# Second aggregation of a graph network layer on one Trainium2 core: the normed rows turned by DMA instead of by TensorE

## The reference, cut to what matters

```
xn = layernorm(x)
x2 = x + gnn(xn, edges) + mix(xn)       # gnn: x @ W0 + b0 + mean_of_neighbours(x) @ W1 + b1, twice
xf = layernorm(x2)
logits = xf @ Wg + bg + bias            # 6250 x 8
top2 -> softmax -> combine
out = x2 + sum over the two experts e of combine[e] * (relu(xf @ W1[e] + b1[e]) @ W2[e] + b2[e])
```

## Time and profile before

| | us |
|---|---|
| median of 3 runs | 2406.96 |
| lowest and highest | 2403.34 to 2407.14 |
| the profiled execution's own time | 2408.94 |
| span of the profile | 2407.4 |

### The profile page before, as it was taken

How to read it: one execution, slowest core, us unless ns; L and a number is a source line. 1 busy time by engine, 2 the same in 40 slices (tenths; PEclk the granted TensorE clock), 3 DMA queues, 4 the chain that set the end, 5 groups by cost and what they waited for, 6 DMA issues and landing times.

```text
span 2407.4 us, 53368 instructions
## 1 busy us (share of the span) xinstructions
PE 2129.6 (88%) x15340; PEld 1320.2 (55%) x15341; DVE 1612.2 (67%) x4900; ACT 1202.9 (50%) x2425; POOL 360.4 (15%) x427
## 2 busy tenths in 40 slices
PE   2555557999999999999799997999999998699997
PEld 2444445555555555555355553444444444599996
DVE  5999999799999999999443342445444455355554
ACT  2445455355555555555545552444444444366664
POOL 1000000000000000000111110111211112266665
PEclk9665667899999999999899998999999999799998
DMA  2111112522222222222222123555555554655553
GB/s 76 44 34 34 34 37 62 167 115 118 109 117 109 120 110 116 117 109 117 102 75 77 50 85 145 193 185 208 187 194 199 186 206 167 165 91 94 87 93 47
DMA packets 132541, 275.61 MB, mean 114 GB/s; under 512 B 30478, under 2 KB 85951, under 8 KB 130291
## 3 DMA queue, kind: packets, MB, share of 16 engines
q1 hardware_dynamic: 104275, 221.29, 26.3%
q0 software_dynamic: 25216, 44.98, 8.5%
q10 hardware_dynamic: 2976, 8.46, 1.1%
HBM read 137.14 MB, written 132.95 MB: 112 GB/s over the span
## 4 chain that ended last, share of the span: by engine, by line
PE 67%; issue 14%; DVE 8%; DVEq 4%; POOLq 2%; POOL 1%; DMA 1%; ACT 1%; ACTq 1%; SPq 0%
PE bank L2107 44%; PE bank L2098 6%; PE bank L2328 6%; PE bank L2313 6%; POOLq L771 2%; DVE big L1027 2%; DVE big L1041 1%; DVEq L1056 1%; DVEq L1024 1%; PE bank L2295 1%; DVEq L1037 1%; PE bank L2115 1%; DVE big L1039 1%; PE bank L1976 1%; DVE R L1000 1%
## 5 line engine op out<-in xcount | busy, mean ns | idle before, releaser
L2107 PE MATMUL bank<-RW,big 128*128 128x512 f16 (+1 forms) x4900 | 1181.4, 380 | 0.0
L2107 PEld LDWEIGHTS bank<-RW,big 128*128 128x128 f16 x4900 | 444.0, 98 | 397.1 <-issue 5.0
L1767 ACT ACTIVATE big<-bank 128x512 f16<-128x512 f32 (+1 forms) x640 | 371.7, 581 | 318.6 <-PE bank L2098 318.6
L1174 DVE TENSOR_TENSOR big<-iotaB,keys 128x512 f16<-128x512 f16 x1300 | 452.2, 418 | 7.9 <-issue 7.8
L2098 PEld LDWEIGHTS bank<-big 128*128 128x128 f16 x2560 | 190.9, 98 | 111.8 <-issue 1.3
L2098 PE MATMUL bank<-big 128*128 128x128 f16 x2560 | 247.5, 219 | 0.3 <-issue 0.3
L892 POOL DMA_INDIRECT out_dram<-big x112 | 179.5, 1602 | 128.5 <-ACT big L1921 94.5
L835 POOL DMA_DIRECT2D big<-in_L_ffn_W_dram x8 | 6.4, 806 | 1147.6 <-DVE R L1233 1144.9
L1912 ACT ACTIVATE big<-bank,b1A,iscA 128x256 f32<-128x256 f32 x224 | 114.3, 560 | 100.2 <-PE bank L2313 94.2
L2313 PE MATMUL bank<-big,RW 128*128 128x256 f16 x1344 | 158.4, 275 | 3.4 <-ACT big L1901 3.4
L2328 PE MATMUL bank<-RW,big 128*128 (+1 forms) x1344 | 155.9, 273 | 0.0
(11 more groups left out here) (396 smaller groups left out, 2931.6 us busy)
## 6 DMA issues: line engine op xcount, KB each, us to landing
big<-a_dram SPq DMA_DIRECT2D x49, 832.0 KB
big<-a_dram SPq DMA_DIRECT2D x49, 768.0 KB, 4.5
a_dram<-big SPq DMA_DIRECT2D x49, 640.0 KB, 3.0
a_dram<-big SPq DMA_DIRECT2D x49, 512.0 KB, 2.6
a_dram<-big SPq DMA_DIRECT2D x49, 448.0 KB, 2.5
big<-rows_dram SPq DMA_DIRECT2D x56, 265.0 KB
big<-in_x_dram SPq DMA_DIRECT2D x96, 128.0 KB, 2.1
big<-in_L_ffn_W_dram POOLq DMA_DIRECT2D x16, 512.0 KB, 4.6
```

Of the source, the lines that this page charges most:

```text
L1174: last = v.tensor_tensor(out[q].rearrange("p b (m k) -> p b m k", k=2), inturn(iotaB[:, :], QB, P // 2), twice(kd[:, q * QB:(q + 1) * QB, ...
L1767: a.activation(Ab[q][:, 0:n], banks[BB(q)][:, 0:n], ACT.Copy).then_inc(s_ab, 1)
L2107: last = mm(bank[:, :], blk(q, c), src, start=(u == 0), stop=(u == T))
```

## The change

The four transposes of a tile on TensorE, the semaphore s_t2 and ScalarE's copy from bank 6 go. ScalarE's turned2 now waits for the low half of the row (s_l2) and for the gate of the tile before (s_lp), runs a one-element activation into a spare word, and issues four DMAs of 128x128 f16 (32 KB each) from its queue, SBUF to SBUF, that transpose on the way; each adds 16 to s_g2. The gate waits for 64 counts a tile, and takes over the waits for s_lr (the last logits were read) and s_cr (the last counts were read). xtg is moved ahead of xrow, to an address that is a multiple of 8 words.

```diff
--- before.py
+++ after.py
@@ -289,8 +289,9 @@
         x2n = sp3b.f32(D)
         x2s, x2m, x2r = sp3b.f32(6), sp3b.f32(2), sp3b.f32(1)
         first_row = sp3b.at
+        sp3b.at = -(-sp3b.at // 8) * 8
+        xtg = sp3b.f16(2 * D)
         xrow = [sp3b.f16(ROWW) for _ in range(2)]
-        xtg = sp3b.f16(2 * D)
         pick = [sp3b.f32(2 * 8).rearrange("p (k n) -> p k n", k=2) for _ in range(2)]
         oneh = [sp3b.f16(8) for _ in range(2)]
         seen = sp3b.f16(8)
@@ -496,7 +497,6 @@
         s_v2 = sem("s_v2")
         s_d2 = sem("s_d2")
         s_n2 = sem("s_n2")
-        s_t2 = sem("s_t2")
         s_h2 = sem("s_h2")
         s_l2 = sem("s_l2")
         s_lp = sem("s_lp")
@@ -1781,9 +1781,13 @@
                     act.wait_ge(s_sx[par], half * 32)
                 a.activation(xrow[par][:, 0:D], x2n, ACT.Copy, scale=S).then_inc(s_h2, 1)
 
-            def turned2(t):
-                act.wait_ge(s_t2, t + 1)
-                a.activation(xtg, bankh[6][:, 0:2 * D], ACT.Copy).then_inc(s_g2, 1)
+            def turned2(t, par):
+                act.wait_ge(s_l2, t + 1)
+                act.wait_ge(s_lp, t)
+                a.activation(cred[:, 1:2], ones[:, 0:1], ACT.Copy)
+                for c in range(4):
+                    act.dma_start_transpose(out=xtg[:, c * P:(c + 1) * P], in_=xrow[par][:, c * P:(c + 1) * P])\
+                       .then_inc(s_g2, 16)
 
             def raise2(t):
                 act.wait_ge(s_lv, t + 1)
@@ -1796,7 +1800,7 @@
                 elif last:
                     deviation(last[0])
                     high2(*last)
-                    turned2(last[0])
+                    turned2(last[0], last[1])
                     raise2(last[0])
                 copy(L, t, bank)
 
@@ -1819,7 +1823,7 @@
                                   w_dram[2:FIRST, :, :].rearrange("e p c -> p e c")).then_inc(s_wf[0], 16)
                     deviation(T - 1)
                     high2(T - 1, 0, (T - 1) // 2)
-                    turned2(T - 1)
+                    turned2(T - 1, 0)
                     raise2(T - 1)
 
             aggregate(0)
@@ -2138,18 +2142,11 @@
                     last = nc.tensor.transpose(banks[6][:, h * P:(h + 1) * P], aggn[:, h * P:(h + 1) * P], ident[:, :])
                 last.then_inc(s_at, 1)
 
-            def transposed2(t, par):
-                pe.wait_ge(s_l2, t + 1)
+            def gate(t):
+
+                pe.wait_ge(s_g2, t * 64 + 64)
                 pe.wait_ge(s_lr, t + 1)
                 pe.wait_ge(s_cr, t + 1)
-                for c in range(4):
-                    last = nc.tensor.transpose(bankh[6][:, c * P:(c + 1) * P], xrow[par][:, c * P:(c + 1) * P],
-                                               ident16[:, :])
-                last.then_inc(s_t2, 1)
-
-            def gate(t):
-
-                pe.wait_ge(s_g2, t + 1)
                 for part in range(2):
                     for k in range(2):
                         last = mm(banks[6][:, D:D + 24], xtg[:, (2 * part + k) * P:(2 * part + k + 1) * P],
@@ -2188,8 +2185,6 @@
                         done.then_inc(s_ap[1], 1)
                     if q == 1 and before:
                         before2(*before)
-                    if q == 7 and last:
-                        transposed2(*last)
                     if q == 9 and last:
                         gate(last[0])
 
@@ -2276,7 +2271,6 @@
             mm(banks[7][:, 0:8], ones[0:1, :], grows[0:1, 2, :], start=True, stop=True).then_inc(s_gp, 1)
             tiles2()
             before2(T - 2, 1)
-            transposed2(T - 1, 0)
             gate(T - 1)
             before2(T - 1, 0)
             pe.wait_ge(s_oneh, T + 1)
```

## The result

Four runs of the changed kernel took 2584.4 to 2591.2 us, median 2586.3, against 2407.1 for the kernel before on the same chips: ratio 1.0744, 95% interval 1.0723 to 1.0766. The change costs 179 us, 7.4%. The forecast was 2518, its range 2425 to 2645.

What follows compares the result with a forecast made beforehand. The prediction took TensorE to bound the kernel. From the profiled 2408.9 us it took 10.6 for transposes and added 92.6 idle, 25 clock and 4 end: 2520, or 2518 against the median; range 2425 to 2645.

Steps and rivals of the forecast that it cites:

- the cover: Between low2's end and the gate: 3.12 us of TensorE matmuls due anyway, within which a wait costs nothing.
- The transposes: On TensorE's chain: removing four a tile saves 0.22 us, 10.6 us over 48 tiles.
- Semaphore and activation: On ScalarE's queue after low2: 0.1 us for semaphore and wake-up, 0.15 us for the one-element activation.
- Issues: On ScalarE's queue: three DMA issues ahead of the last at 0.60 us each, 1.80 us; from below 1.35.
- Landing: From the last turning DMA's issue until its data arrive, for which the gate waits: 3.0 us.
- Idle a tile: TensorE waiting before the gate: 5.05 us from low2 to landing less 3.12, so 1.93 us, 92.6 us over 48 tiles.
- The clock: TensorE's granted clock drops after gaps in one tile in four: 12 tiles at 2.1 us, 25 us.
- The end: Last tile's gate, with nothing to hide the wait and 2 MB of weights ahead in the queue: +4 us.
- ScalarE, SP, POOL: Other engines' work in the tile loop, exp, matrix loads and scatters: delays there stay hidden and cost nothing.
- That all fits under the cover: Rival at the gate: low2 to landing within about 3.12 us, so 2404 or 2400 us in all; chance 0.11.
- A landing like that of a quiet transfer: Rival at the gate: landing 2.0 us, idle 0.93 a tile, no clock lost, 2446 us; chance 0.16 for 2410 to 2455.
- The four in a row: Rival at the gate: each turn lands before the next moves, idle 5.13 us a tile, 2650 to 2750; chance 0.25 above 2590.

## Why the prediction was right, and what was off

The sign, the place and the mechanism came out as put: the cover between low2 and the gate, an excess paid 48 times, a gap that costs some tiles the clock, a longer tail. The size was 179 us where I had 111. One of the prediction's own signs of being wrong came true: the issues were far over 0.7 us. Term by term:

- **The transposes.** Right: 10.6 us forecast, and the kernels that turn by DMA without a wait have a period of 10.95, which is 10 us less over the stage.
- **The cover.** 3.12 us forecast, 3.33 measured, for the 0.21 us between weight load and matmul. In favour of the change.
- **Semaphore and activation.** 0.25 us forecast; the first issue began 0.04 us after low2's end, beside the activation.
- **Issues.** This is the term that was mis-sized. I took 0.60 us from plain issues in the earlier trace rows for three of them, 1.80; they took 3.7 (1785.72 to 1789.46). These 1.9 us are more than the whole miss of 1.3 us in the time from low2 to the gate. The bounds in the text (from 1.35 up) came from plain issues too, so the upper end of this term was too low. That 2586 us still lies inside the forecast's own band, 4 us under its top of 2590, is in part luck: the landing and the wake-up were put 0.8 us too high, and made up for nearly half of what the issues were short. One issue of 128x512 shows that it is a price of the instruction; SyncE's queue shows that it is not ScalarE's.
- **Landing.** 3.0 us from its issue forecast, 2.4 measured for the last of the four (1789.46 to 1791.85) and 2.8 for one of 128x512. I took it high because the DMA engines were 94% busy when the turns start. By the prediction's own terms the last issue comes at 1751.18 + 0.25 + 1.80 = 1753.2, and there have them at 0.01.
- **Idle a tile.** Low2 to gate 6.2 to 6.4 us against 5.05; idle 13.93 - 10.95 = 2.98 us against 1.93, 143 us against 93. The 123.2 us of wait in the profile of the changed kernel are less, since matmuls at the lower clock fill a part of the gap there.
- **The clock.** 25 us forecast, 12 tiles at 2.1; 41 to 44 measured, in 33 of the 48 tiles at 1.3 in the mean. Count and price were both off, in opposite directions. From the earlier trace rows I had read that the level fell 2.1 us after the last matmul, and with a gap of 1.93 expected to stand just short of it. With the later gate TensorE's idle before the gate was 1.8 us at most and the column stayed full; in the changed kernel it was 1.8 to 3.1 and most tiles lost it. The gap was mis-sized, and the number of tiles with it. But 2.1 us is no edge either: the clock was at its lower level after a gap of 1.90 (the gate at 1731.94, clock 0.57 in the 2 us behind it) and full after one of 3.04 (1747.78, clock 1.00).
- **The end.** +4 forecast, +5.4 measured, for the reason given, the 2 MB in the same queue. Putting them behind the turn gave 4 us back in the profile of the kernel with one issue.
- **ScalarE, SP, POOL.** Their cover held: TensorE waits for nothing in the stage but the turns (the row of waits above).

The sum with the measured terms: 143 + 44 - 10 + 5.4 - 2.0 = 180, against 181.5 between the spans.

The rivals. That all fits under the cover was false for this kernel, and true for the same work in one instruction; its condition, low2 to landing under 3.1 to 3.3 us, was the right one. A landing like that of a quiet transfer was half right: 2.4 us is near the 2.0 of the earlier trace rows, but it was not the landing that was mis-sized most. The Trainium skill (Advanced Engine Details and Errata, section X-Bar Transpose (TRN2)) says that turning DMAs are as fast as ordinary ones. For the landing the trace comes near it, 2.4 us beside the 2.0 of the earlier trace rows; for the issue it does not, 1.22 us beside 0.36 on one queue. The four in a row were nearest to the truth, not since each waits for the landing of the one before, but since the queue issues them one after another. The Trainium skill (VectorE: DVE Perf Modes, section The three transpose paths) gives 1309 ns for one such turn; the trace agrees for the time in the queue, 1.27 us a turn, but the turned data are there only 2.4 us after an issue begins. The 2540 us that I had worked out from it left out the landing behind the last issue. Its 390 ns for TensorE are not what is paid here: 0.22 us for four on the chain.

## What to carry to other kernels

Price an operation that the trace does not show by more than its plain relatives: the turning DMA's issue cost nearly twice the dearest plain one in the rows I had taken, and four of them stood in a row in a loop that had 3.3 us of room. A DMA that has a fixed price of issue is worth issuing once: where four instructions lose 179 us, the same turn in one is as fast as the kernel before (ratio 0.9985, 0.9969 to 1.0000), and 0.5% faster with the 2 MB load behind the last turn. When a wait enters a pipelined loop, look for what stands between it and the end of the loop and behind what it queues: a later gate gave back 93 us, a load moved behind the last turn 4 in the profile.

## What the runs showed of the hardware

- A transposing DMA from SBUF to SBUF held its queue for 1.27 us on ScalarE and 1.22 on SyncE, for 32 KB as for 128 KB (1.22), and landed 2.4 to 2.8 us after its issue began.
- 196 such turns beside a matrix traffic of 1.6 MB a tile changed the time by less than the measurement tells apart (ratio 1.0000, 0.9988 to 1.0011).
- A turn behind a load of 2 MB in the same queue let the gate start only 6.3 us after its issue; with the load behind it the same turn took 2.4.
- With TensorE idle for 1.8 us at most before each gate, in tiles of 12.9 us, the granted clock stayed full. With 1.8 to 3.1 us, in tiles of 13.5 to 16.1, it was at the lower level behind 33 of the 48 gates, which cost up to 2.1 us on ten matmuls of 128x512 (4.57 us from gate to copy instead of 2.46). A gap of 1.90 us was followed by the lower level and one of 3.04 was not. So the length of the gap alone does not tell whether a tile loses it.
